# The routed pair sums of a mixture-of-experts layer: from GpSimd to VectorE, one chunk ahead

## What is computed

```python
scores = jax.nn.softmax((xt @ gate_w.T).astype(jnp.float32), axis=-1)
_, idx = jax.lax.top_k(scores + gate_bias, TOPK)
weights = jnp.take_along_axis(scores, idx, axis=1).astype(x.dtype)
y = jnp.zeros_like(xt)
for e in range(N_EXPERTS):
    gate_e = jnp.sum(jnp.where(idx == e, weights, 0.0), axis=1)
    h = jax.nn.silu(xt @ w1[e].T) * (xt @ w3[e].T)
    y = y + gate_e[:, None] * (h @ w2[e].T)
z = jax.nn.silu(xt @ sw1.T) * (xt @ sw3.T) @ sw2.T
return (y + z).reshape(shape)
```

## Time and profile before

| | |
|---|---|
| median of 3 runs | 622.0 us (621.9 to 622.91) |
| the profiled execution | 621.86 us, its span 620.1 us |
| mean granted clock of TensorE | 0.957 of full speed |
| busy over the span: PE, DVE, ACT, POOL | 552.9, 441.1, 329.1, 291.3 us |
| YG loads: 16 x 512 KB, issue to landing | median 8.8 us |
| out stores: 32 x 128 KB, issue to landing | median 1.9 us |

### The profile page before, as it was taken

One profiled execution on the slowest core, in us unless ns is written; L12 is line 12 of the kernel. 1 busy time (PEld: TensorE's weight loads), 2 busy tenths in 40 slices (PEclk: granted clock), 3 DMA queues, 4 the chain that ended last, 5 costly groups with the idle time before them and its releaser, 6 DMA issues.

```text
span 620.1 us, 11503 instructions
## 1 busy us (share of the span) xinstructions
PE 552.9 (89%) x3468; PEld 480.1 (77%) x3468; DVE 441.1 (71%) x1202; ACT 329.1 (53%) x684; POOL 291.3 (47%) x593
## 2 busy tenths in 40 slices
PE   5869899977989969819999998999999999998874
PEld 4856799876589965508888886888888888887764
DVE  7949998594987756686767644666666666664895
ACT  3548997265998616414454432555555555554221
POOL 4047500206730016017767661466666766665690
PEclk9979899997989988958999999999999999999998
DMA  8999000000000039002222222233333333331994
GB/s 259 325 305 45 2 1 2 2 0 1 1 2 1 1 99 403 9 17 97 87 79 96 88 95 57 71 108 106 104 104 105 105 106 104 106 101 61 336 335 142
DMA packets 57129, 63.03 MB, mean 102 GB/s; under 512 B 14736, under 2 KB 50448, under 8 KB 57072
## 3 DMA queue, kind: packets, MB, share of 16 engines
q1 hardware_dynamic: 49216, 43.75, 24.8%
q0 software_dynamic: 6480, 17.90, 8.2%
q10 hardware_dynamic: 1376, 0.66, 0.4%
HBM read 30.64 MB, written 31.65 MB: 100 GB/s over the span
## 4 chain that ended last, share of the span: by engine, by line
PE 55%; DVE 6%; issue 1%; ACT 1%; POOL 0%; DVEq 0%; POOLq 0%
PE bank L1314 16%; PE bank L1316 15%; PE bank L1315 15%; PE bank L1437 3%; PE bank L1453 2%; PE bank L1322 1%; PE bank L1366 1%; DVE h_lo L1244 1%; DVE XN L1088 1%; DVE X L1227 0%; PE bank L1339 0%; DVE mv L1085 0%; DVE X L1217 0%; DVE hf L1236 0%; DVE XT_lo L1126 0%
## 5 line engine op out<-in xcount | busy, mean ns | idle before, releaser
L970 POOL DMA_INDIRECT token_out<-YS,to_row x71 | 71.7, 1010 | 54.0 <-DVE back L1281 49.8
L934 POOL DMA_INDIRECT slots_in<-X,slot x64 | 66.3, 1036 | 60.0 <-DVE slot L1201 30.4
L676 PE MATMUL a_bank<-VO,E_hi 128*128 128x258 f32 x272 | 78.5, 289 | 3.5 <-issue 1.8
L680 PE MATMUL a_bank<-VO,E_lo 128*128 128x258 f32 x272 | 78.5, 288 | 0.0
L678 PE MATMUL a_bank<-VO,E_hi 128*128 128x256 f32 x272 | 78.2, 288 | 0.0
L1270 DVE TENSOR_TENSOR hr<-bank,sr 128x256 f32<-128x256 f32 x71 | 30.1, 424 | 60.9 <-ACT sr L1047 60.9
L1314 PE MATMUL bank<-W_hi,XST_hi 128*128 x142 | 62.4, 439 | 0.5 <-DVE XST_lo L1286 0.5
L1047 ACT ACTIVATE sr<-bank 128x256 f32<-128x256 f32 x71 | 27.2, 383 | 64.7 <-PE bank L1316 64.7
L1021 ACT ACTIVATE h_hi<-hf 128x512 fp32r<-128x512 f32 x32 | 20.2, 632 | 73.1 <-DVE hf L1236 73.1
L1316 PE MATMUL bank<-W_hi,XST_lo 128*128 x142 | 57.1, 402 | 0.0
L1315 PE MATMUL bank<-W_lo,XST_hi 128*128 x142 | 56.8, 400 | 0.0
(11 more groups left out here) (247 smaller groups left out, 1675.3 us busy)
## 6 DMA issues: line engine op xcount, KB each, us to landing
XS<-slots_in SPq DMA_DIRECT2D x71, 131.0 KB, 2.0
slots_in<-blank SPq DMA_DIRECT2D x7, 1179.0 KB, 14.9
YG<-token_out SPq DMA_DIRECT2D x16, 512.0 KB, 8.8
W_raw<-in_wT_dram SPq DMA_DIRECT2D x8, 768.0 KB, 13.6
X<-in_x_dram SPq DMA_DIRECT2D x8, 512.0 KB, 8.4
out_dram<-X SPq DMA_DIRECT2D x32, 128.0 KB, 1.9
token_out<-YS,to_row POOLq DMA_INDIRECT x71, 2.5
slots_in<-blank SPq DMA_DIRECT2D x1, 1048.0 KB, 14.3
```

The source lines that it names most:

```text
L676: pe.matmul(O_ps[Q % 2][j][:, 0:D + 2], E_hi[:, n % NE, cols], VO[:, kt, 0:D + 2], start=(kt == 0), stop=False)
L680: mm = pe.matmul(O_ps[Q % 2][j][:, 0:D + 2], E_lo[:, n % NE, cols], VO[:, kt, 0:D + 2], start=False, stop=(kt == qt))
L934: pool.indirect_dma_start(out=xs, out_offset=bass.IndirectOffsetOnAxis(ap=slot[k][:, t:t + 1], axis=0), in_=X[:, t, :], in_offset=None).th ...
L970: pool.indirect_dma_start(out=ys, out_offset=bass.IndirectOffsetOnAxis(ap=to_row[:, i:i + 1], axis=0), in_=YS[:, i % NYS, :], in_offset=No ...
```

## The change

GpSimd's loop of pair sums is taken out. The same 16 additions are written in VectorE's program as `add_pairs(g)`, which waits for the group's loads. The new table `pairs_to_add` puts them behind `hf` and the `add_routed` of a chunk and ahead of its `h_lo`: group 0 in chunk 25, group 1 in 26, group 2 in 27, groups 3 and 4 in 28, group 5 in 29, 6 in 30 and 7 in 31. The table `group_to_add` is altered so that `add_routed` comes one chunk after the sum: groups 3 and 4 in chunk 29 (before: 3 in 29, 4 in 30), group 5 in 30 and group 6 in 31 (before: 5 and 6 in 31).

```diff
         def group_to_add(n):
 
-            return {2: [0], 3: [1], 4: [2], 5: [3], 6: [4], 7: [5, 6]}.get(n - MC * HALF, [])
+            return {2: [0], 3: [1], 4: [2], 5: [3, 4], 6: [5], 7: [6]}.get(n - MC * HALF, [])
+
+        def pairs_to_add(n):
+
+            return {1: [0], 2: [1], 3: [2], 4: [3, 4], 5: [5], 6: [6], 7: [7]}.get(n - MC * HALF, [])
...
-            for g in range(NG):
-                pool.wait_ge(s_yg[g], 16 * TOPK)
-                for h in range(0, GT, 2):
-                    tiles = slice(g * GT + h, g * GT + h + 2)
-                    pool.tensor_tensor(YG[:, tiles, 0, :], YG[:, tiles, 0, :], YG[:, tiles, 1, :], ALU.add)\
-                        .then_inc(s_yy, 1)
...
+            def add_pairs(g):
+
+                dve.wait_ge(s_yg[g], 16 * TOPK)
+                for h in range(0, GT, 2):
+                    tiles = slice(g * GT + h, g * GT + h + 2)
+                    dve.tensor_tensor(YG[:, tiles, 0, :], YG[:, tiles, 0, :], YG[:, tiles, 1, :], ALU.add)\
+                       .then_inc(s_yy, 1)
+
...
                         if G >= HALF:
                             for g in group_to_add(n):
                                 add_routed(g)
+                            for g in pairs_to_add(n):
+                                add_pairs(g)
                         dve.wait_ge(s_hh, n + 1)
```

## The result

The changed kernel takes 619.4 us (median of 5 runs, 618.8 to 619.9) against 622.0 us (median of 5, 621.48 to 623.23). The ratio is 0.9953, with a 95% interval of 0.994 to 0.9967. Executed again later beside the kernel before, it took 619.62 against 623.16 us (medians of 8 and 13), ratio 0.9947 (0.9928 to 0.9965). The forecast was 618.7 us, with a range of 617.2 to 620.9.

The account below looks back on a forecast made before the run. VectorE, working in order, was taken to set the end through `h_lo`. Last `h_lo` at 609.12 plus 7.7 us gives a span of 616.8; adding 1.76 and 0.14 gives 618.7 us, range 617.2 to 620.9.

Parts of the forecast that it names:

- Part 1, the stretch: VectorE's last stage: without GpSimd's sums, `add_routed` loses 5.5 us, `h_lo` 4.0 and `XN` 2.9, together 12.4 us.
- Part 2, the price of a sum: VectorE's 16 added pair sums: 0.61 us each, taken from `add_routed`, 9.8 us in all.
- neither bound: Limits for one pair sum on VectorE: lower about 0.34 us, upper about 1.70 from start to start.
- The rule against the change: Work may be moved off a saturated VectorE; by this, the sums would be 9.8 us more on VectorE.
- Part 3, the path: Chunks 25 to 31, worked forward through VectorE and TensorE: last `h_lo` starts at 609.12 us, before 612.42; span 3.3 us shorter.
- The stretch stays: Slower rival: transfers, not GpSimd, lengthen VectorE's work; 7.6 us more, 629.6 us; 6% together with dear sums.
- Small costs at the waits: Even rival: late loads, or 1 to 1.5 us more at each of two TensorE waits; 620.8 to 622.5; even rivals 11% together.
- The stores become the end: Even rival: if the store rate falls by a fifth, stores set the end near 621 us; even rivals 11% together.
- a dear sum: Pair sums on VectorE: gain gone at 1.02 us each, over 0.2% slower from 1.18; 6% together with the stretch staying.

## Why the prediction was right

**The bound and its cause.** That VectorE sets the end through `h_lo`, and that GpSimd's sums make its instructions dear, held in the run that took GpSimd's reads away (sums left out, 684 ns) and in the one that put them back (reads of no use, 888 to 996 ns).

**Part 1, the stretch.** Forecast 12.4 us removed. After, `add_routed` takes 10.2 in place of 15.7 us, `h_lo` 5.5 in place of 9.4, `XN` of group 7 1.38 in place of 4.28: 5.5 + 3.9 + 2.9 = 12.3 us.

**Part 2, the price of a sum.** Forecast 0.68 us long and 0.61 to the next; measured 685 ns, two in 1.29 and four in 2.49 us. The nearest row, `add_routed`, was the right one, and neither bound was needed. The rule against the change (don't load a full VectorE) failed here since a share of what filled VectorE was waiting.

**Part 3, the path.** From `hf` of chunk 24 to the last `h_lo` the sum gives 609.12 - 574.51 = 34.61 us; measured 34.56 and 34.51. The waits of TensorE were to be 1.8, 1.15 and 2.6 us; idle stood 1.56, 0.91 and 2.42, always some 0.2 less, since the trace counts idle time from a matmul's end, and a matmul of 0.39 us ends 0.16 us behind its slot of 0.23. The part behind the last `h_lo` was 7.5 us in place of 7.7. No wait for loads appeared behind group 0's. One sentence of the prediction's account was too dear: the eight sums of chunks 28, 29 and 31 don't add 0.61 us each, 4.9 us, over a kernel without sums, but 3.0 (34.56 - 31.56), since part of them fills slack. The sum of the path, which follows TensorE and VectorE in turn, had this right.

**What was off.** The median came out 0.7 us above the forecast. In the profiled execution the term is the part ahead of the stage, which the prediction took as fixed from one execution: 571.27 us in that one, 572.60 in the changed kernel's, 570.6 to 573.1 us over the study for kernels with the same code there. That this also moved the median is not shown. The 3.3 us of the stage are there; ratios of 0.9953 and 0.9947 amount to 2.9 and 3.3 us, and the interval of the first (2.1 to 3.7 us) holds the forecast.

**The rivals.** "The stretch stays" fell with the sums left out. "Small costs at the waits" did not occur: the stage came out within 0.1 us of the sum. "The stores become the end" did not occur. That a dear sum would turn the gain round holds in kind: with each sum twice the kernel is 0.6% slower than before.

## What to carry to other kernels

Where one engine's equal instructions have two prices in a trace, look for what the other engine did at the dear ones, and above all for a short gap in it; then an engine that is busy all the time may have room for more work, if that work silences the other. Here 10 us of additions moved onto a full VectorE saved 3.3 us. Afterwards place such work by the waits that are left: behind what the next engine waits for, and in the idle time at the end, which gave another 2.3 us in the stage.

## What the runs showed of the hardware that I had not expected

A GpSimd fill of 3.5 us held up each of four small VectorE instructions (SBUF to SBUF, one tensor input) for about its whole length, 16.12 us for work of 1.4; the same fills in eighths cost 1.2 us in the profiled execution; and neither delayed VectorE's additions of two SBUF tensors by anything (683 and 679 ns). I had expected this kind, but not its size. And from 15 to 17.5 us one and the same program ran at the full clock in one execution and at 0.53 of it in another. Its second block began 1.4 us later in the latter and its last stage 0.9 us later: as much as many a change.
